# A 64-state selective scan on one core: y's sums in 64x64 tiles, odd states with exchanged halves, carries copied on GpSimd, preparation one pair later

## The chip, the cores and the metric

The program runs on 1 core of a Trainium2 chip. The metric is the device time of one execution in microseconds (us). The engines of the core work through queues of their own and wait for each other by semaphores: PE (TensorE, matmuls), DVE (VectorE), ACT (ScalarE), POOL (GpSimd), and SP, which only issues transfers. PEld is the loading of weights into PE.

## The reference

The network is four layers on x of shape 4 x 128 x 64 x 64: a sparse attention, a selective scan with 64 states, a rank-one attention and a two-way scan with 16 states. The change is in the second layer, whose core, per sample (L = 4096 positions, C = 128 channels, n = 64 states), is this:

```python
xproj = xp @ W_in                              # u and the convolution's input
...                                            # layer norm of u with gamma, beta
dt, B_, C_ = split(u @ W_dt)                   # 8 + 64 + 64 columns
delta = softplus(dt @ W_dtr + b_dtr)
a = exp(delta[..., None] * A)                  # A = -exp(A_log), one value per channel and state
h[l] = a[l] * h[l-1] + delta[l] * B_[l] * u[l] # for each of 64 states
y[l] = sum over states of C_[l, n] * h[l, :, n]  + D * u[l]
y = y + silu(conv) * ...                       # gated 3x3 depthwise convolution
out = y @ W_out + x
```

## The kernel before, in words

Channels lie on the 128 partitions, positions along the free dimension. The scan layer (`scan_layer`, L455 on) takes the 16384 positions of the four samples in 16 **chunks** of 1024 (index K; four to a sample), and in each chunk the 64 states one after the other. A state in a chunk is a **unit**; two units, an even and an odd one, are a **pair** (index k, 0 to 31). Every engine runs an unrolled program written pair by pair, so the order of each queue is the order of its source.

For each pair:

- ACT makes `decay` for the two units: exp(delta * A), one 128x1024 activation each (L829), and scales eight blocks of the transposed `duT` by the odd unit's B (L842), giving `xt`.
- PE broadcasts the even unit's row of B to all partitions with one-hot weights `sel` (L668, `broadcast_B`) and transposes `xt` back (L678, `turn_back`). DVE multiplies the broadcast B by `du` in place (L1036, `even_input`).
- DVE scans the even and the odd unit (L1049, 2.3 us each), reading the input from PSUM and writing `h`. In three chunks of four it then copies the last column of each `h` into `carry` (L1055, `keep`), from which the next chunk's scan of that state starts.
- SP loads the unit's row of C, broadcast to 128 partitions, into one of `CS` = 5 slots of `hc`; POOL multiplies it by `h` (L951, `product`).
- PE adds the product into `y_sum` (two PSUM banks) with an identity matrix as weights (L688, `add_state`): two 128x512 float32 matmuls a unit, which the profile shows as four. PE adds the products of the pair before the one that DVE is at.

Between these, each engine prepares the next chunk in pieces, tied to k: PE projects u (L566, k = 0, 1), POOL squares it into `usq` (L914, k = 1), PE sums the squares over channels with eight one-column matmuls (L573, `prep_var`, k = 4), DVE and ACT make the reciprocal root (L990 to L1000, L758, L760, k = 4), PE broadcasts it (L583, k = 5, 6), DVE scales u (L1005, k = 5, 6), and further projections, delta's softplus on ACT and POOL (POOL's four steps after pairs 18 to 21) and the transposed du follow. The finished chunk is closed by `add_y` (L1023, DVE, after the scans of pair 0 of the next chunk), the gating (L1017), `add_conv` (L946, POOL, after pair 2), the projection (L659) and the residual (L1029). PE also makes the 3x3 convolution in 18 pieces between pairs (L644).

PE's wait for the squares stands ahead of everything that follows it in PE's queue: the sums and the broadcast of B for the next pair.

The fourth layer (`two_way_scan_layer`) is a scan of the same shape with 16 states. It already forms y's sums in four 64x64 tiles (L1545, `add_pair`), takes exp(delta * A) of the odd states from a copy of delta with exchanged halves (`crossed`), and keeps carries on DVE (L1927).

Of the kernel before, what the change touches and what calls it, by code (L numbers as in the profile page):

```python
# [454 lines left out]
def scan_layer(nc, x, w, sel, weights_in, conv_weights):  # L455
# [11 lines left out]
    HS, DS, CS, XS = 4, 4, 5, 4  # L467
    ctx = ExitStack()
    with ctx:
# [12 lines left out]
        delta = sb("delta", [128, 2, CH])  # L482
        du = sb("du", [128, 2, CH])
# [7 lines left out]
        part = sb("part", [PARTS * SEL, CH], BF16)  # L491
        z1, z2 = sb("z1", [128, CH]), sb("z2", [128, CH])
        z3, rows_sb = usq, z1[0:S1, :]
        carry = sb("carry", [128, S1])
# [27 lines left out]
        c_in = [sem(f"c_in_{i}") for i in range(CS)]  # L522
        hc_done = sem("hc_done"); sum_mm = sem("sum_mm"); y_out = sem("y_out"); yg_ready = sem("yg_ready")
# [15 lines left out]
        def _(sp):  # L539
# [11 lines left out]

            sp.dma_start(conv_raw, conv_weights).then_inc(conv_in, 16)
            store_rows(0)
            for K in range(NCH):
                for q in range(S1):
                    load_row(K, q)
                    if q == 26 and K + 1 < NCH:
                        store_rows(K + 1)

        @block.tensor  # L560
        def _(pe):
# [99 lines left out]
            def broadcast_B(P, p):  # L661
# [49 lines left out]
            for K in range(NCH):  # L711
                p = K % 2
                for k in range(PAIRS):
                    P = K * PAIRS + k
                    turn_back(P)
                    if P:
                        add_state(2 * P - 2)
                    if k in CONV:
                        convolution(K, *CONV[k])
                    if K + 1 < NCH:  # L720
                        if k < 2:
                            prep_u(K + 1, k)
                        if k == 4:
                            prep_var(K + 1)
                        if k in (5, 6):
                            prep_rstd(K + 1, k - 5)
# [16 lines left out]
            for unit in range(NCH * S1 - 2, NCH * S1):  # L743
                add_state(unit)
# [4 lines left out]
        def _(act):  # L749
# [25 lines left out]
            def split_high(K):  # L775
                act.wait_ge(bdt_out, 2 * K + 2)
                nc.scalar.activation(part[:], rest[0:PARTS * SEL, :], ACT.Identity,
                                     scale=w[0:PARTS * SEL, L1_AT["below_top"]][:, 0:1]).then_inc(part_ready, 1)

            def split_middle(K):  # L780
                act.wait_ge(rest_ready, K + 1)
                nc.scalar.activation(part[:], rest[0:PARTS * SEL, :], ACT.Identity,
# [22 lines left out]
            def soft_log(K):  # L805
# [3 lines left out]
                nc.scalar.activation(z3[:], z3[:], ACT.Identity, bias=wt("minus_one")).then_inc(exp_ln, 1)  # L809
                nc.scalar.activation(z2[:], z1[:], ACT.Ln, bias=1.0).then_inc(exp_ln, 1)  # L810

            def duT_copy(K, p, j):
                act.wait_ge(duT_mm, 2 * K + j + 1)
                nc.scalar.activation(duT[:, p, 4 * j:4 * j + 4, :].rearrange("p t d -> p (t d)"), prep_ps,
                                     ACT.Identity).then_inc(duT_out, 1)
# [8 lines left out]
            def decays(unit, p):  # L824
                K, q = divmod(unit, S1)
                if q == 0:
                    act.wait_ge(delta_ready, K + 1)
                at_least(act, scan_done, unit - DS + 1)
                nc.scalar.activation(decay[:, unit % DS, :], delta[:, p, :], ACT.Exp,  # L829
# [41 lines left out]
            for K in range(NCH):  # L871
                p = K % 2
                for k in range(PAIRS):
# [10 lines left out]
                    if K + 1 < NCH:  # L884
                        if k < 2:
                            u_copy(K + 1, 1 - p, k)
                        if k == 4:
# [1305 lines left out]
```

## Time and profile before

| | us |
|---|---|
| median of 3 runs (lowest, highest) | 10606.26 (10604.6, 10616.05) |
| the profiled execution: its own time | 10616.89 |
| its span | 10615.1 |
| the scan layer: first scan to the last `add_y` | 2838.8 to 5945.1 |

| engine | busy us | share of the span |
|---|---|---|
| PE | 9717.4 | 92% |
| DVE | 8515.8 | 80% |
| ACT | 8057.9 | 76% |
| POOL | 5905.9 | 56% |

Times in the rows are from the start of the span. The profiled execution is 10.6 us above the median; what is worked out from its rows is a difference and is laid on the median. Matmuls overlap one another, so their starts tell more than their durations; DVE's instructions overlap the one before by about 0.08 us. PEclk is the share of full speed that TensorE's clock was granted: 1.0 is 2.4 GHz, 0.5 is 1.2 GHz.

### The profile page before, as it was taken

How to read it: one execution, taken by the hardware profiler on the slowest of the kernel's cores; microseconds unless marked ns; L12 is line 12 of the kernel's file. 1: busy time of each engine (PE TensorE's matmuls, PEld its weight loads, DVE VectorE, ACT ScalarE, POOL GpSimd, SP SyncE). 2: the span in 40 equal slices, each digit the busy share in tenths (PEclk: the TensorE clock that was granted, in tenths of full speed). 3: DMA queues.
4: the chain of work that ended last, by engine and by line, in shares of the span. 5: the costliest groups of instructions: out<-in, count | busy, mean ns of one | idle time of the engine just before them, and what ended most of it. 6: DMA issues, size and time to landing. Idle time of an engine off the chain costs nothing. (4 is left out here: it accounts for less than half of the span.)

```text
span 10615.1 us, 137498 instructions
## 1 busy us (share of the span) xinstructions
PE 9717.4 (92%) x45956; PEld 5177.6 (49%) x45956; DVE 8515.8 (80%) x8102; ACT 8057.9 (76%) x14637; POOL 5905.9 (56%) x2628
## 2 busy tenths in 40 slices
PE   9999999999899999999999999988888888888885
PEld 6767767677444444444444444433333333333332
DVE  7858858578599999999999411159999999999997
ACT  5646646466488888888888555579999998888885
POOL 0000000000288888888888300058989988889885
PEclk9999999999899999999999999989999999999997
DMA  1000000000145555545555100035555555555556
GB/s 41 0 1 0 0 0 0 0 0 0 61 173 175 175 175 174 177 174 174 176 174 177 66 8 8 8 120 184 186 184 179 187 182 189 184 186 188 183 187 220
DMA packets 335957, 1241.58 MB, mean 117 GB/s; under 512 B 38672, under 2 KB 38800, under 8 KB 331792
## 3 DMA queue, kind: packets, MB, share of 16 engines
q1 hardware_dynamic: 335472, 1235.51, 34.7%
q8 instruction: 256, 4.19, 0.2%
q14 instruction: 229, 1.88, 0.1%
HBM read 1145.18 MB, written 56.62 MB: 113 GB/s over the span
## 5 line engine op out<-in xcount | busy, mean ns | idle before, releaser
L951 POOL TENSOR_TENSOR l_hc<-l_h,l_hc 128x1024 f32<-128x1024 f32 x1024 | 2398.8, 2365 | 451.5 <-DVE l_h L1049 451.0
L1841 POOL TENSOR_TENSOR l_ring<-l_ring 128x1024 f32<-128x1024 f32 x1024 | 2429.7, 2397 | 347.4 <-DVE l_ring L1919 341.3
L1919 DVE TENSOR_TENSOR_SCAN l_ring<-l_ring,l_carry,l_ps 128x1024 f32<-128x1024 f32 x960 | 2200.1, 2333 | 1.3
L688 PE MATMUL l_ps<-l_hc,w_sb 128*128 128x512 f32 x4096 | 1936.4, 595 | 69.1 <-POOL l_hc L951 61.7
L1049 DVE TENSOR_TENSOR_SCAN l_h<-l_decay,l_carry,l_ps 128x1024 f32<-128x1024 f32 x768 | 1760.3, 2334 | 4.3 <-issue 0.4
L1545 PE MATMUL l_ps<-l_ring,w_sb 64*64 64x512 f32 x8192 | 1216.9, 667 | 343.0 <-POOL l_ring L1841 334.4
L116 POOL COPY l_qm<-l_q 128x128 f32 x128 | 82.7, 648 | 2576.4 <-PE l_ps L188 2179.5
L829 ACT ACTIVATE l_decay<-l_delta,w_sb 128x1024 f32<-128x1024 f32 x1024 | 1152.8, 1138 | 168.8 <-DVE l_h L1049 168.6
L1731 ACT ACTIVATE l_xt<-l_duT,l_BT 128x128 f32<-128x128 f32 x4096 | 1246.0, 388 | 0.0
L842 ACT ACTIVATE l_xt<-l_duT,l_BT 128x128 f32<-128x128 f32 x4096 | 1245.9, 388 | 0.0
L212 PE MATMUL l_ps<-l_attnT,l_vT 128*128 128x128 f32 x8192 | 1095.7, 277 | 1.3 <-ACT l_attnT L283 1.3
L212 PEld LDWEIGHTS l_ps<-l_attnT,l_vT 128*128 128x128 f32 x8192 | 1013.9, 192 | 138.0 <-issue 114.7
L188 PE MATMUL l_ps<-l_k,l_qm 128*128 128x512 f32 x2048 | 1055.0, 599 | 16.7 <-DVE l_E L395 16.6
L688 PEld LDWEIGHTS l_ps<-l_hc,w_sb 128*128 128x128 f32 x4096 | 735.3, 190 | 659.6 <-issue 491.8
L1184 PE MATMUL l_ps<-l_E,l_hs 128*128 128x512 f32 x2048 | 880.0, 592 | 5.2 <-DVE l_hs L1250 5.2
L401 DVE SCALAR_TENSOR_TENSOR l_E<-l_relu,l_E 128x1024 f32<-128x1024 f32 x512 | 626.7, 1225 | 287.2 <-ACT l_E L276 287.2
L276 ACT ACTIVATE l_E<-l_E,l_offsets 128x1024 f32<-128x1024 f32 x512 | 587.0, 1146 | 290.5 <-DVE l_E L395 290.4
L270 ACT ACTIVATE l_relu<-l_ps,l_offsets 128x1024 f32<-128x1024 f32 x512 | 570.8, 1115 | 272.6 <-PE l_ps L188 270.8
L1211 ACT ACTIVATE l_E<-l_g,l_neg_max,l_f 128x4096 f32<-128x4096 f32 x128 | 486.4, 3800 | 380.2 <-PE l_ps L1184 368.3
L1903 DVE TENSOR_TENSOR l_ps<-l_du,l_ps 128x1024 f32<-128x1024 f32 x512 | 622.2, 1215 | 179.9 <-PE l_ps L1518 178.4
L1528 PEld LDWEIGHTS l_ps<-w_sb,l_xt 128*128 128x128 f32 x4096 | 479.0, 150 | 556.4 <-DVE l_ring L1919 385.0
L201 PEld LDWEIGHTS l_ps<-w_sb,l_E 128*128 128x128 f32 x4096 | 507.1, 141 | 409.8 <-issue 392.7
(233 smaller groups left out, 15001.6 us busy)
## 6 DMA issues: line engine op xcount, KB each, us to landing
l_hc<-l_rows_dram SPq DMA_DIRECT2D x1024, 512.0 KB, 3.7
l_ring<-l_rows_dram SPq DMA_DIRECT2D x1024, 512.0 KB, 4.8
l_crossed<-l_delta SPq DMA_DIRECT2D x128, 256.0 KB, 5.3
l_gate_dram<-l_gate SPq DMA_DIRECT2D x32, 512.0 KB, 7.1
l_recon_dram<-l_recon SPq DMA_DIRECT2D x32, 512.0 KB, 5.4
l_gate<-l_gate_dram SPq DMA_DIRECT2D x32, 512.0 KB, 6.0
l_xw<-x_dram SPq DMA_DIRECT2D x30, 513.5 KB, 7.3
x_dram<-x SPq DMA_DIRECT2D x16, 512.0 KB, 2.6
```

Source lines behind the costliest of these rows:

```text
L188: ins = nc.tensor.matmul(logits[c % 2][:, j * BANK:(j + 1) * BANK], qm[:, h, :], k[:, c * CH + j * BANK:c * CH + (j + 1) * BANK], start=Tr ...
L212: ins = nc.tensor.matmul(ps[:, bank, 0:128], vT[:, t * 128:(t + 1) * 128], attnT[:, g % 2, j * 128:(j + 1) * 128], start=t == 0, stop=t == ...
L688: ins = nc.tensor.matmul(y_sum[:, half(j)], ident, hc[:, unit % CS, half(j)], start=q == 0, stop=q == S1 - 1)
L829: nc.scalar.activation(decay[:, unit % DS, :], delta[:, p, :], ACT.Exp, scale=wt("A")[:, q:q + 1]).then_inc(decay_ready, 1)
L842: ins = nc.scalar.activation(xt[:, (2 * P + hf) % XS, t * 128:(t + 1) * 128], duT[:, p, blk, :], ACT.Identity, scale=BT[:, p, blk, k:k + 1])
L951: nc.gpsimd.tensor_tensor(hc[:, unit % CS, :], h[:, unit % HS, :], hc[:, unit % CS, :], ALU.mult).then_inc(hc_done, 1)
L1049: nc.vector.tensor_tensor_scan(h[:, unit % HS, :], decay[:, unit % DS, :], odd_in if odd else even_in, before, ALU.mult, ALU.add).then_inc ...
L1184: ins = nc.tensor.matmul(ps[:, j, :], hs[:, s, :], E[:, s, j * BANK:(j + 1) * BANK], start=start, stop=stop)
L1545: ins = nc.tensor.matmul(ps[to, 4 + j, :], ident[own, own], hc[own, (2 * P + odd) % CS, half(j)], start=r == 0 and phase == 0, stop=r == P ...
L1731: ins = nc.scalar.activation(xt[:, (2 * P + hf) % XS, t * 128:(t + 1) * 128], duT[:, S % 2, 4 * hf + t, :], ACT.Identity, scale=BT[:, K % ...
L1841: nc.gpsimd.tensor_tensor(hc[:, unit % CS, :], h[:, unit % HS, :], hc[:, unit % CS, :], ALU.mult).then_inc(hc_done, 1)
L1919: nc.vector.tensor_tensor_scan(h[:, unit % HS, order], decay[:, unit % DS, order], x_now[:, order], before, ALU.mult, ALU.add).then_inc(sc ...
```

## The change

1. **y's sums.** `add_state` becomes `add_pair(P, phase)`. Each of its two phases issues four 64x64-tile matmuls of 64x512, one for each combination of input half and output half of the partitions, for both units of a pair. The odd unit's halves are exchanged, so that its channels 0 to 63 lie on partitions 64 to 127. The sums are two pairs late instead of one, and `hc` has 7 slots instead of 5.
2. **Exchanged halves.** The decay of odd units comes from `crossed`, a copy of delta with exchanged halves that SP makes with two transfers of 256 KB a chunk (`cross_delta`, queued behind the row load of unit 62); `duT_copy` writes exchanged halves; A's odd columns are rolled by 64.
3. **Carries** are copied by POOL, ahead of each product, instead of by DVE.
4. **Preparation.** PE's and ACT's pieces for u move from k = 0, 1 to 2, 3; POOL's squares from after pair 1 to after pair 4; `prep_var`, `rstds` and `newton` from 4 to 5; the scaling by one; `add_y` from after pair 0 to after pair 1 and `add_conv` from after pair 2 to after pair 3.
5. **sel** keeps one column a state and is read with a stride of 0 for the 128 columns of weights, in the scan layer and in the fourth layer. `part` shares memory with `z2`, with two more waits on ACT for that.

```diff
-    HS, DS, CS, XS = 4, 4, 5, 4
+    HS, DS, CS, XS = 4, 4, 7, 4
...
+            def cross_delta(K):
+                sp.wait_ge(delta_ready, K + 1)
+                at_least(sp, decay_ready, S1 * K)
+                for side in range(2):
+                    sp.dma_start(crossed[64 * side:64 * side + 64, :],
+                                 delta[64 - 64 * side:128 - 64 * side, K % 2, :]).then_inc(crossed_in, 16)
...
-                    ins = nc.tensor.matmul(even_in[:, half(j)], sel[:, k * 128:(k + 1) * 128], stack[:, p, half(j)],
+                    ins = nc.tensor.matmul(even_in[:, half(j)], sel[:, k:k + 1].broadcast_to([PARTS * SEL, 128]), stack[:, p, half(j)],
...
-            def add_state(unit):
-                K, q = divmod(unit, S1)
-                if q == 0:
-                    at_least(pe, y_out, K)
-                pe.wait_ge(hc_done, unit + 1)
-                for j in range(2):
-                    ins = nc.tensor.matmul(y_sum[:, half(j)], ident, hc[:, unit % CS, half(j)], start=q == 0,
-                                           stop=q == S1 - 1)
-                ins.then_inc(sum_mm, 1)
+            def add_pair(P, phase):
+
+                K, k = divmod(P, PAIRS)
+                if phase == 0:
+                    if k == 0:
+                        at_least(pe, y_out, K)
+                    pe.wait_ge(hc_done, 2 * P + 2)
+                    at_least(pe, sum_mm, 2 * P)
+                else:
+                    pe.wait_ge(first_half_mm, P + 1)
+                lower, upper = slice(0, 64), slice(64, 128)
+                for own, other, j in ((lower, upper, phase), (upper, lower, 1 - phase)):
+                    for odd, to in enumerate((own, other)):
+                        ins = nc.tensor.matmul(ps[to, 4 + j, :], ident[own, own], hc[own, (2 * P + odd) % CS, half(j)],
+                                               start=k == 0 and phase == 0, stop=k == PAIRS - 1 and phase == 1)
...
                     turn_back(P)
-                    if P:
-                        add_state(2 * P - 2)
...
-                        if k < 2:
-                            prep_u(K + 1, k)
-                        if k == 4:
+                        if k in (2, 3):
+                            prep_u(K + 1, k - 2)
+                        if k == 5:
                             prep_var(K + 1)
...
+                    if P > 1:
+                        add_pair(P - 2, 0)
                     if P + 1 < NCH * PAIRS:
                         broadcast_B(P + 1, p if k + 1 < PAIRS else 1 - p)
-                    if P:
-                        add_state(2 * P - 1)
...
+                    if P > 1:
+                        add_pair(P - 2, 1)
...
             def product(unit):
+                K, q = divmod(unit, S1)
+                pool.wait_ge(scan_done, unit + 1)
+                if K % NC < NC - 1:
+                    nc.gpsimd.tensor_copy(carry[:, q:q + 1], h[:, unit % HS, CH - 1:CH]).then_inc(kept, 1)
                 pool.wait_ge(c_in[unit % CS], 16 * (unit // CS) + 16)
-                pool.wait_ge(scan_done, unit + 1)
...
-                    if k == 2 and K:
+                    if k == 3 and K:
                         add_conv(K - 1)
                     if K + 1 < NCH:
-                        if k == 1:
+                        if k == 4:
                             squares(K + 1, 1 - p)
```

PE's queue around the squares' sum, before, in the first chunk: pairs 3 to 5. L688 are the sums of y, L668 the broadcast of B, L678 the transposes, L573 the squares' sum.

```order
L678 MATMUL l_ps<-w_sb,l_xt 128x128 x8
L688 MATMUL l_ps<-l_hc,w_sb 128x512 x2
L573 MATMUL l_ps<-w_sb,l_usq 128x1 x8
L668 MATMUL l_ps<-l_stack,sel 128x512 x2
L688 MATMUL l_ps<-l_hc,w_sb 128x512 x2
L678 MATMUL l_ps<-w_sb,l_xt 128x128 x8
```

The same place after: L690 are the transposes, L585 the squares' sum, L707 the sums of y, L680 the broadcast of B.

```order
L690 MATMUL l_ps<-w_sb,l_xt 128x128 x8
L585 MATMUL l_ps<-w_sb,l_usq 128x1 x8
L707 MATMUL l_ps<-l_hc,w_sb 64x512 x4
L680 MATMUL l_ps<-l_stack,sel 128x512 x2
L707 MATMUL l_ps<-l_hc,w_sb 64x512 x4
```

The squares' sum now stands in the group of pair 5 (before: of pair 4), and behind it both phases of a pair's sum enclose the broadcast of B.

POOL's queue from the end of the first chunk into the second, before: L951 are products, L914 squares u, L946 is `add_conv`.

```order
L951 TENSOR_TENSOR l_hc<-l_h,l_hc 128x1024 x24
L914 TENSOR_TENSOR l_usq<-l_u 128x1024
L951 TENSOR_TENSOR l_hc<-l_h,l_hc 128x1024 x2
L946 TENSOR_TENSOR l_yg<-l_yg,l_cg 128x1024
```

The same after, from the products of pair 3 of the second chunk: L979 copies a carry, L981 is a product, L973 `add_conv`, L941 the squares.

```order
L979 COPY l_carry<-l_h 128x1
L981 TENSOR_TENSOR l_hc<-l_h,l_hc 128x1024
L979 COPY l_carry<-l_h 128x1
L981 TENSOR_TENSOR l_hc<-l_h,l_hc 128x1024
L973 TENSOR_TENSOR l_yg<-l_yg,l_cg 128x1024
L979 COPY l_carry<-l_h 128x1
L981 TENSOR_TENSOR l_hc<-l_h,l_hc 128x1024
L979 COPY l_carry<-l_h 128x1
L981 TENSOR_TENSOR l_hc<-l_h,l_hc 128x1024
L941 TENSOR_TENSOR l_usq<-l_u 128x1024
```

Before, the squares come behind pair 1 and three pairs ahead of the pair in which PE asks for them; after, they come behind `add_conv` and pair 4, one pair ahead.

DVE's queue at the start of the second chunk, before: L1049 are scans, L1036 `even_input`, L1055 the copies of carries, L1023 `add_y`.

```order
L1049 SCALAR_TENSOR_TENSOR l_h<-l_decay,l_carry,l_ps 128x1024 x2
L1023 SCALAR_TENSOR_TENSOR l_yg<-l_u,w_sb,l_ps 128x1024
L1036 TENSOR_TENSOR l_ps<-l_du,l_ps 128x1024
L1055 COPY l_carry<-l_h 128x1 x2
L1049 SCALAR_TENSOR_TENSOR l_h<-l_decay,l_carry,l_ps 128x1024 x2
```

After: L1079 are scans, L1066 `even_input`, L1053 `add_y`, L1047 the gating.

```order
L1079 SCALAR_TENSOR_TENSOR l_h<-l_decay,l_carry,l_ps 128x1024 x2
L1066 TENSOR_TENSOR l_ps<-l_du,l_ps 128x1024
L1079 SCALAR_TENSOR_TENSOR l_h<-l_decay,l_carry,l_ps 128x1024 x2
L1053 SCALAR_TENSOR_TENSOR l_yg<-l_u,w_sb,l_ps 128x1024
L1066 TENSOR_TENSOR l_ps<-l_du,l_ps 128x1024
L1047 SCALAR_TENSOR_TENSOR l_cg<-l_ps,w_sb,l_cg 128x512
```

`add_y` stands one pair later, and the copies of carries are gone from DVE.

## Rows read from the trace of the kernel before

**Rows 1.** Stretches: length, busy us of each engine, PEclk, DMA.

```profile
2838.00:5945.00 3107.00, 2971.46 (x10930) 1527.59 (x10930) 3046.91 (x2500) 2626.25 (x5546) 2657.90 (x1144) 1.00 0.51 174
7012.00:10530.00 3518.00, 2956.94 (x15906) 1147.36 (x15906) 3292.42 (x2714) 3212.97 (x6215) 3133.73 (x1338) 0.94 0.57 184
```

**Rows 2.** DVE's waits in chunks 1 to 14: us, times, longest.

```profile
DVE l_ps L1036 <- PE l_ps L668: 22.8, 45, 0.9
DVE l_yg L1023 <- PE l_ps L688: 11.3, 15, 0.9
```

**Rows 3.** DVE in order of time, chunk 7: start, us, instruction, [idle before].

```profile
4203.86 1.28 DVE L1023 SCALAR_TENSOR_TENSOR l_yg<-l_u,w_sb,l_ps 128x1024 f32<-128x1024 f32 x1 [0.86 <-PE l_ps L688]
...
4206.32 4.58 DVE L1049 TENSOR_TENSOR_SCAN l_h<-l_decay,l_carry,l_ps 128x1024 f32<-128x1024 f32 x2
...
4212.59 4.58 DVE L1049 TENSOR_TENSOR_SCAN l_h<-l_decay,l_carry,l_ps 128x1024 f32<-128x1024 f32 x2
4217.08 1.21 DVE L1036 TENSOR_TENSOR l_ps<-l_du,l_ps 128x1024 f32<-128x1024 f32 x1
4218.33 4.59 DVE L1049 TENSOR_TENSOR_SCAN l_h<-l_decay,l_carry,l_ps 128x1024 f32<-128x1024 f32 x2
```

**Rows 4.** DVE, two pairs of chunk 6 between which two copies of carries stand.

```profile
4023.79 4.58 DVE L1049 TENSOR_TENSOR_SCAN l_h<-l_decay,l_carry,l_ps 128x1024 f32<-128x1024 f32 x2
...
4029.54 4.59 DVE L1049 TENSOR_TENSOR_SCAN l_h<-l_decay,l_carry,l_ps 128x1024 f32<-128x1024 f32 x2
```

**Rows 5.** POOL in order of time, chunk 7, from the products of pair 1.

```profile
4208.81 4.70 POOL L951 TENSOR_TENSOR l_hc<-l_h,l_hc 128x1024 f32<-128x1024 f32 x2 [3.23 <-DVE l_h L1049]
4213.46 1.90 POOL L914 TENSOR_TENSOR l_usq<-l_u 128x1024 f32<-128x1024 f32 x1
...
4219.97 2.35 POOL L946 TENSOR_TENSOR l_yg<-l_yg,l_cg 128x1024 f32<-128x1024 f32 x1
4222.29 9.29 POOL L951 TENSOR_TENSOR l_hc<-l_h,l_hc 128x1024 f32<-128x1024 f32 x4
```

**Rows 6.** PE at granted clock 1.0: the scan layer's squares' sum; layer four.

```profile
4226.52 1.84 PE L573 MATMUL l_ps<-w_sb,l_usq 128*128 128x1 f32 x16
4228.23 0.59 PE L668 MATMUL l_ps<-l_stack,sel 96*128 96x512 bf16 x2
...
7879.09 1.09 PE L1545 MATMUL l_ps<-l_ring,w_sb 64*64 64x512 f32 x8
7880.11 0.60 PE L1518 MATMUL l_ps<-l_stack,sel 96*128 96x512 bf16 x2
...
7881.66 1.09 PE L1528 MATMUL l_ps<-w_sb,l_xt 128*128 128x128 f32 x8
```

**Rows 7.** PE behind long gaps: layer four, and the squares' sum ahead of chunk 0.

```profile
2786.59 3.55 PE L573 MATMUL l_ps<-w_sb,l_usq 128*128 128x1 f32 x16 [2.75 <-POOL l_usq L914]
...
10390.96 1.98 PE L1545 MATMUL l_ps<-l_ring,w_sb 64*64 64x512 f32 x8 [4.62 <-POOL l_ring L1841]
10392.88 1.04 PE L1518 MATMUL l_ps<-l_stack,sel 96*128 96x512 bf16 x2
...
10395.76 1.75 PE L1528 MATMUL l_ps<-w_sb,l_xt 128*128 128x128 f32 x8
```

**Rows 8.** Small POOL instructions: in order of time, and one line's (ns min/median/max).

```profile
0.27 0.10 POOL L2186 MEMSET const-float32-1.0<- 128x1 f32 x1
...
L116 POOL COPY l_qm<-l_q x128: 291/541/4263, 22.6 to 2659.0; 128x128 f32 x128
```

**Rows 9.** Weight loads: layer four's sel (busy us, mean ns | idle before), and L170 (ns min/median/max).

```profile
L1518 PEld LDWEIGHTS l_ps<-l_stack,sel 96*128 96x128 bf16 x1024 | 59.4, 99 | 560.5 <-DVE l_ring L1919 307.5 <-issue 252.9
...
L170 PEld LDWEIGHTS l_ps<-w_sb,l_rinv x256: 185/190/192, 44.5 to 2123.4; 128*128 128x128 f32 x128
```

**Rows 10.** DMA issues of the page: count, KB each, median us to landing.

```profile
l_crossed<-l_delta SPq DMA_DIRECT2D x128, 256.0 KB, 5.3
```

More of the change, by code:

```diff
@@ L482, in scan_layer @@
         delta = sb("delta", [128, 2, CH])
+        crossed = sb("crossed", [128, CH])
         du = sb("du", [128, 2, CH])
@@ L558, in _ @@
                         store_rows(K + 1)
+                    if q == 62 and K + 1 < NCH:
+                        cross_delta(K + 1)
         @block.tensor
@@ L738, in _ @@
                         project(K - 1, k - 21)
+                    if P > 1:
+                        add_pair(P - 2, 0)
                     if P + 1 < NCH * PAIRS:
                         broadcast_B(P + 1, p if k + 1 < PAIRS else 1 - p)
-                    if P:
-                        add_state(2 * P - 1)
-            for unit in range(NCH * S1 - 2, NCH * S1):
-                add_state(unit)
+                    if P > 1:
+                        add_pair(P - 2, 1)
+            for P in (NCH * PAIRS - 2, NCH * PAIRS - 1):
+                for phase in range(2):
+                    add_pair(P, phase)
             for j in range(2):
@@ L776, in split_high @@
                 act.wait_ge(bdt_out, 2 * K + 2)
-                nc.scalar.activation(part[:], rest[0:PARTS * SEL, :], ACT.Identity,
+                at_least(act, low_ready, 2 * K)
+                nc.scalar.activation(part, rest[0:PARTS * SEL, :], ACT.Identity,
                                      scale=w[0:PARTS * SEL, L1_AT["below_top"]][:, 0:1]).then_inc(part_ready, 1)
@@ L781, in split_middle @@
                 act.wait_ge(rest_ready, K + 1)
-                nc.scalar.activation(part[:], rest[0:PARTS * SEL, :], ACT.Identity,
+                nc.scalar.activation(part, rest[0:PARTS * SEL, :], ACT.Identity,
                                      scale=w[0:PARTS * SEL, L1_AT["below_top"]][:, 1:2]).then_inc(part_ready, 1)
@@ L813, in duT_copy @@
                 act.wait_ge(duT_mm, 2 * K + j + 1)
-                nc.scalar.activation(duT[:, p, 4 * j:4 * j + 4, :].rearrange("p t d -> p (t d)"), prep_ps,
-                                     ACT.Identity).then_inc(duT_out, 1)
+                nc.scalar.activation(duT[:, p, 4 * j:4 * j + 4, :].rearrange("p t (s d) -> p t s d", s=2)[:, :, ::-1, :],
+                                     prep_ps.rearrange("p (t s d) -> p t s d", t=4, s=2), ACT.Identity).then_inc(duT_out, 1)
             def silu(K, j):
@@ L827, in decays @@
                     act.wait_ge(delta_ready, K + 1)
+                if q == 1:
+                    act.wait_ge(crossed_in, 32 * K + 32)
                 at_least(act, scan_done, unit - DS + 1)
-                nc.scalar.activation(decay[:, unit % DS, :], delta[:, p, :], ACT.Exp,
+                nc.scalar.activation(decay[:, unit % DS, :], crossed[:] if q % 2 else delta[:, p, :], ACT.Exp,
                                      scale=wt("A")[:, q:q + 1]).then_inc(decay_ready, 1)
@@ L1080, in _ @@
                     scan(P, 1)
-                    if k == 0 and K:
+                    if k == 1 and K:
                         add_y(K - 1, 1 - p)
@@ L1517, in broadcast_B @@
                     for j in range(2):
-                        ins = nc.tensor.matmul(even_in[:, half(j)], sel[:, r * 128:(r + 1) * 128], stack[:, K % 2, half(j)],
+                        ins = nc.tensor.matmul(even_in[:, half(j)], sel[:, r:r + 1].broadcast_to([PARTS * SEL, 128]), stack[:, K % 2, half(j)],
                                                start=True, stop=True)
@@ L2054, in network @@
         sem = lambda name: ctx.enter_context(nc.semaphore(name))
-        sel = ctx.enter_context(nc.sbuf_tensor("sel", [PARTS * SEL, SEL * 128], BF16))
+        sel = ctx.enter_context(nc.sbuf_tensor("sel", [PARTS * SEL, SEL], BF16))
         x_dram = nc.dram_tensor("x_dram", [C, B * N], F32, kind="Internal").ap()
@@ L2125, in layer1_arrays @@
                ("out_w", 0, W_out), ("ident", 0, _np.eye(128)), ("ones", 0, _np.ones((128, 1))),
-               ("A", 0, A_log[:, by_unit]), ("below_top", 0, below_top), ("minus_one", 0, _np.full((128, 1), -1)),
+               ("A", 0, _np.where(_np.arange(S1) % 2, _np.roll(A_log[:, by_unit], 64, 0), A_log[:, by_unit])),
+               ("below_top", 0, below_top), ("minus_one", 0, _np.full((128, 1), -1)),
                ("bdt_b", 0, column(_np.concatenate([b_dt[even_B]] * PARTS + [b_dt[:R1]]))),
@@ L2167, in one_hot_rows @@
 def one_hot_rows():
-    select = _np.zeros((PARTS * SEL, SEL, 128), _np.float32)
-    for a in range(PARTS):
-        for i in range(SEL):
-            select[a * SEL + i, i, :] = 1
-    return select.reshape(PARTS * SEL, SEL * 128).astype(mybir.dt.np(BF16))
+    return _np.concatenate([_np.eye(SEL)] * PARTS).astype(mybir.dt.np(BF16))
 def kernel(**inputs):
```

40 lines of the change are left out of this document (20 added, 20 removed).

## The prediction

> **What bounds the kernel now.** I read the stretches first [rows 1]: in the scan layer DVE is busy for 3047 of 3107 us, PE for 2971, POOL for 2658, and PE's clock is granted in full. DVE sets the pace, PE follows closely. Then DVE's own waits [rows 2]: in the 14 chunks 1 to 14 it waits 45 times for the broadcast of B (22.8 us) and 15 times for y's sums (11.3 us). Last, DVE in order of time: a plain pair takes 4218.33 - 4212.59 = 5.74 us from scan to scan [rows 3]. With two copies of carries in it, it takes 4029.54 - 4023.79 = 5.75 us [rows 4]: the copies lie in the time that the scan must wait for `even_input` anyway. So the engine that the change relieves most, PE, is not the bound; it can give back no more than the waits.
>
> **What the change can give.** Chunks 1 to 14: the recorded waits are 34.1 us. Each of these 60 also loses the 0.08 us by which DVE's instructions otherwise overlap, 4.8 us. Delays too short to be listed are some 0.5 us a chunk by the starts of chunk 7, 7 us. Without the copies, a gating, scaling or transposed copy can start 0.12 us earlier at six places in a chunk: 0.7 us in the 11 of these chunks that have copies, 8 us. Together 54 us. Chunk 0 has the same kinds of waits, 3.6 us; the last chunk's pairs run without a wait, so it gives nothing, and its tail pays 0.9 us since two pairs of sums are left instead of one. **Gain: 57 us**, if nothing new is late.
>
> The saving on PE is real but hidden. A phase of tile matmuls advances PE by 7880.11 - 7879.09 = 1.02 us [rows 6]. Two phases, a broadcast (0.6) and the transposes (1.09) make 3.7 of a pair's 5.74 us: 2 us are then idle, or 1 where a piece of preparation or convolution stands between.
>
> **What is late next: the squares.** POOL now squares u behind `add_conv` and the products of pair 4, and PE asks for it in pair 5, ahead of the sums and of the broadcast of B for pair 6. I follow a chunk without copies, from its first scan at 0. Pair 1 scans at 5.74. `add_y` (1.28 less 0.08 of overlap) now stands behind it, and the gating adds 4212.59 - 4206.32 - 5.74 = 0.53 [rows 3], so pair 2 scans at 5.74 + 5.74 + 1.20 + 0.53 = 13.21, pair 3 at 18.95, pair 4 at 24.69, pair 5 at 30.43. `even_input` for pair 6 would follow 4217.08 - 4212.59 = 4.50 later, **at 34.93**.
>
> POOL starts a pair's products 4208.81 - 4206.32 = 2.49 after its scans begin and takes 4213.46 - 4208.81 = 4.65 for the two [rows 3, 5]. Pair 3: 21.44 to 26.09. `add_conv` takes 4222.29 - 4219.97 = 2.32: to 28.41. Pair 4, whose first scan has long ended: to 33.06. Squares, 1.90: **34.96**. PE has had nothing to do since its transposes of pair 5, which end about 30.3: a gap of 4.7 us.
>
> Behind the squares stand, on the way to `even_input`: the squares' sum (1.71 from its start to the next, at full clock), a phase (1.02), the broadcast (0.60) [rows 6]. At full clock that ends at 38.3: a stall of 3.4 us.
>
> But after a gap of 4.62 us the fourth layer's phase took 1.98 us instead of 1.09 and the broadcast 1.04 instead of 0.60, and 4.8 us in, the transposes still took 1.75 instead of 1.09 [rows 6, 7]: PE ran at 1.2 GHz for some 6.3 us. Ahead of chunk 0, after a gap, the squares' sum itself took 3.55 us instead of 1.84 [rows 7]. With those, the chain is 3.45 + 1.92 + 1.03 = 6.40, which is about as long as the slow spell, and the last of it ends at 41.4: **a stall of 6.5 us**. If the clock came back after the squares' sum it would be 5.2. I take 6.5, since the gap is as long as the one in the row and one-column matmuls are the lightest work PE has here.
>
> **The copies on POOL** (price c each) delay the squares by four of them. The trace has no such copy. A 128x1 MEMSET on POOL takes 0.10 us; L116's copy of 128 columns has a median of 0.54 [rows 8]. I take 0.10, by the form that is nearest in size; the ends are 0.03 (the pitch at which the MEMSETs follow each other) and 0.54. In a plain pair POOL is idle for 5.74 - 4.65 = 1.09 us, so two copies cost DVE nothing there up to 0.54. So the stall in a chunk with copies is 6.5 + 0.4 = 6.9.
>
> The Trainium skill, GPSIMD Engine Reference, section Elementwise, side-by-side cycle accounting, gives DVE about 156 ns of dispatch an instruction and GpSimd two software hops where DVE has one. As an estimate from that page a copy would be near 0.31 us, and the sum would grow by 4 x 0.21 x 11 = 9 us; no trace here shows it.
>
> Chunk 0 has no `add_conv` and no `add_y`: its squares end 2.49 + 4.65 + 1.90 + 0.2 = 9.24 after pair 4's scans, the chain at 15.7, against 10.24 for `even_input`: 5.4 us. Chunk 15 prepares nothing. **Cost: 3 x 6.5 + 11 x 6.9 + 5.4 = 101 us.**
>
> **What is hidden.** POOL's four delta steps after pairs 18 to 21 each add 2.3 us to a pair that leaves 1.09 free: the products come 4.9 us late, 5.7 with the copies, less about 1 that DVE spends there itself. A product must be done when the scan four units on begins, 11.5 us after its own scan; begun at 2.5 and 2.3 long, it may be 6.7 late. That holds up to c of about 0.3. The two transfers for `crossed` land 5.3 us after issue [rows 10]. SP can issue them when the chunk's last decay is made; `decay` has four slots, so ACT makes that one nearly two pairs ahead of its scan, and the first decay that reads `crossed` is wanted by the scan two units further: 5.3 us within some 13. A row of C for an odd unit can only be asked for when the pair three before is summed, at about the start of its own pair, and is needed 6 us in: a landing like that of [rows 10] leaves 1 us. The new wait of `split_high` is for work of a chunk ago, that of the logarithm for a POOL step two pairs ago. The carries' wait is met two pairs early.
>
> The Trainium skill, TensorEngine Tiling (Array Packing), section Key Properties, says that changing the tiling mode drains TensorE. The change brings four such changes a pair. The rows differ: in layer four a broadcast starts 1.02 after the phase begins, as tightly as between equal forms [rows 6], so nothing is added for it.
>
> `sel` read with a stride of 0: a load of it takes 99 ns, a float32 load from a broadcast column 190 as any float32 load [rows 9]. I take no change. At worst 0.09 us on each of the fourth layer's 512 broadcasts, 46 us; where DVE does not wait for them, nothing.
>
> **Sum:** 101 - 57 = +44 us on the profiled execution's 10616.9; laid on the median of 10606.3: **10650 us**.
>
> **Rivals.**
> - *The clock stays up* (not slower). If PE's clock is not lowered in the gap, or is back at once, the chain is 3.3 us: 3 x 3.4 + 11 x 3.8 + 2.7 = 55 against 57: 10604 us. It decides below a stall of 3.8 us a chunk. For it: layer four's clock is granted at 0.94 on the whole [rows 1], so most of its gaps cost nothing. Against it: gaps of this length [rows 7].
> - *PE's wait for the squares binds nothing* (faster), if the squares are ready before 31: the gain of 57 alone, 10549 us. Against it: pair 4's second product can't start before 29.2 and squares 1.9 follow it. It would need POOL's order to be other than its source.
> - *Dear copies.* At c = 0.54 POOL needs 64 x (2.33 + 0.54) + 18 = 202 us a chunk (its two instructions by their pitch, 18 for the other steps) and becomes the bound, against 3107/16 = 194.2 now: 11 x 7.6 us and a few more, about +86 us, 10692. It begins to bind at c of about 0.3.
> - *Slower weight loads* from `sel`: up to 46 more, 10655 to 10696.
> - *A low clock in ordinary pairs.* PE is idle for 2 us in each, as in layer four. Where its clock falls, a pair with a piece of preparation needs about 7 us instead of 5.74; with two or three a chunk, +50 us: 10700. For it: 0.94 [rows 1]; against it, that the gaps are of 1.5 us.
>
> **How the numbers follow.** Forecast 0.56: 10650, itself from 10625 (clock back early) to 10665. Clock stays up 0.13. Faster 0.07. Dear copies 0.09. Weight loads 0.08. Low clock elsewhere 0.07. The range that holds 8 in 10 is 10602 to 10692: it leaves out the faster case and the upper parts of the last three. About 0.2% (21 us) is what a measurement of this kernel can tell from no change; above 10627 lie all of the forecast but 0.04 and the last three cases: slower 0.52 + 0.24 = 0.76; within 0.2%: 0.13 + 0.04 = 0.17; faster 0.07.
>
> **What would show it.** DVE's wait for the broadcast of B should be 15 waits of about 6.5 to 7 us (5.4 the first), all before pair 6, and nearly no others; the wait for y's sums gone. PE should wait some 4.7 us for POOL's squares, its sum take about 3.5 us and the granted clock there be 0.5. The copies on POOL should last about 0.1 us. PE's busy time in the scan layer should fall by hundreds of us to no effect. Stalls of 3.4 would refute the clock; none would refute the order; waits of DVE for POOL's products around pairs 20 to 24 would show dear copies; more of DVE's waits for B in layer four, slower loads.

## The result, and the profile after

The changed kernel takes 10643.03 us (median of 10 runs, 10636.49 to 10658.11), the kernel before 10604.69 us beside it (10 runs, 10598.11 to 10616.05): a ratio of 1.0036, 95% interval [1.0026, 1.0046]. It is slower by 38 us. The profiled execution has a span of 10656.0 us, 40.9 more than before.

The same two stretches as in [rows 1] (length, busy us of PE, PEld, DVE, ACT and POOL, PEclk, DMA):

```profile
2838.00:6000.00 3162.00, 2500.99 (x15046) 982.08 (x15045) 3017.68 (x1745) 2642.10 (x5553) 2752.84 (x1913) 0.96 0.53 174
7012.00:10570.00 3558.00, 2975.51 (x15958) 1161.00 (x15960) 3308.65 (x2716) 3232.12 (x6235) 3141.14 (x1343) 0.94 0.56 182
```

In the scan layer PE has lost 470 us of work, and the layer has become longer. DVE's waits in the first stretch say why (us, times, longest), beside those of [rows 2]:

```profile
DVE l_ps L1066 <- PE l_ps L680: 126.2, 17, 24.6
DVE l_tmp L1024 <- ACT l_root L783: 8.3, 15, 0.6
...
DVE l_yg L1053 <- PE l_ps L707: 5.3, 1, 5.3
```

The wait of 24.6 us stands ahead of the first scan, as before. The other 16 make 101.6 us: one of 0.38, and 15 that are one wait a chunk. The wait for y's sums is gone but for the last chunk's. PE in order of time, chunk 7 (start, us, instruction, [idle before]), for [rows 6, 7]:

```profile
4244.76 1.09 PE L690 MATMUL l_ps<-w_sb,l_xt 128*128 128x128 f32 x8 [0.61 <-DVE l_h L1079]
4250.44 3.54 PE L585 MATMUL l_ps<-w_sb,l_usq 128*128 128x1 f32 x16 [4.60 <-POOL l_usq L941]
4253.92 1.98 PE L707 MATMUL l_ps<-l_hc,w_sb 64*64 64x512 f32 x8
4255.84 1.03 PE L680 MATMUL l_ps<-l_stack,sel 96*128 96x512 bf16 x2
```

The granted clock in 4250.4 to 4258.0 is 0.50, that is 1.2 GHz, behind a gap of 4.60 us. POOL, for [rows 5], and DVE, for [rows 3], in the same chunk:

```profile
4236.80 4.70 POOL L981 TENSOR_TENSOR l_hc<-l_h,l_hc 128x1024 f32<-128x1024 f32 x2 [1.06 <-DVE l_h L1079]
4241.44 2.38 POOL L973 TENSOR_TENSOR l_yg<-l_yg,l_cg 128x1024 f32<-128x1024 f32 x1
4243.76 4.69 POOL L981 TENSOR_TENSOR l_hc<-l_h,l_hc 128x1024 f32<-128x1024 f32 x2
4248.38 1.92 POOL L941 TENSOR_TENSOR l_usq<-l_u 128x1024 f32<-128x1024 f32 x1
```

```profile
4245.86 4.58 DVE L1079 TENSOR_TENSOR_SCAN l_h<-l_decay,l_carry,l_ps 128x1024 f32<-128x1024 f32 x2
4256.91 1.23 DVE L1066 TENSOR_TENSOR l_ps<-l_du,l_ps 128x1024 f32<-128x1024 f32 x1 [6.46 <-PE l_ps L680]
4258.05 0.16 DVE L1020 TENSOR_SCALAR l_var<-l_ps 128x8 f32<-128x8 f32 x1
4258.76 0.17 DVE L1024 TENSOR_TENSOR l_tmp<-l_var,l_root 128x8 f32<-128x8 f32 x1 [0.55 <-ACT l_root L783]
4259.00 0.17 DVE L1026 TENSOR_TENSOR l_tmp<-l_tmp,l_root 128x8 f32<-128x8 f32 x1
```

POOL goes without a pause through the products of pair 3, `add_conv`, the products of pair 4 and the squares, which end at 4250.30; PE's chain behind them (the squares' sum, a phase of y's sums, the broadcast) ends at 4256.87, and only then can DVE make the input of pair 6.

In what follows, "the layer" is the time from the first scan of the scan layer to the start of its last `add_y`: 3106.3 us before, 3140.6 after, so +34.3. Until layer four's first scan it is then 4.0 us less, in layer four (first scan to last `add_y`) 8.4 us more. Layer four's code is the same in all the variants below that keep the change, and there it took from 3504.4 to 3527.6 us in the profiled executions, so the 8.4 is no finding.

The clock falls in ordinary pairs too. In 2838 to 5945 of the kernel before it was never below 1.0; in the same stretch after the change it is 0.50 for 232 us in all, and some 70 of them are not at a stall. In chunk 7, for example, it is 0.50 in 4232.1 to 4235.5, where PE had idled 2.25 us and then worked; the transposes there last 1.97 us. In the changed kernel DVE waits for none of this: outside the 15 stalls its only wait for the broadcast is the one of 0.38 us.

### The profile page after: what moved, and what is told of

Same layout as the page of the kernel before. It is cut to its first block and busy times, and to the rows that moved or that the text cites. A ratio compares the mean times of both kernels' runs of the same rounds, so it can differ in the third digit from the quotient of the medians.

```text
span 10656.0 us, 145495 instructions
## 1 busy us (share of the span) xinstructions
PE 9227.2 (87%) x50052; PEld 4629.1 (43%) x50052; DVE 8487.8 (80%) x7334; ACT 8068.5 (76%) x14637; POOL 5993.8 (56%) x3396
## 3 DMA queue, kind: packets, MB, share of 16 engines
q1 hardware_dynamic: 338032, 1243.12, 35.7%
q14 instruction: 225, 1.84, 0.1%
## 5 line engine op out<-in xcount | busy, mean ns | idle before, releaser
L981 POOL TENSOR_TENSOR l_hc<-l_h,l_hc 128x1024 f32<-128x1024 f32 x1024 | 2414.1, 2363 | 122.1 <-DVE l_h L1079 113.2
L1079 DVE TENSOR_TENSOR_SCAN l_h<-l_decay,l_carry,l_ps 128x1024 f32<-128x1024 f32 x768 | 1760.0, 2333 | 11.2
L707 PE MATMUL l_ps<-l_hc,w_sb 64*64 64x512 f32 x8192 | 1151.4, 633 | 2.7 <-POOL l_hc L981 2.2
L690 PE MATMUL l_ps<-w_sb,l_xt 128*128 128x128 f32 x4096 | 581.1, 287 | 281.6 <-DVE l_h L1079 279.5
L690 PEld LDWEIGHTS l_ps<-w_sb,l_xt 128*128 128x128 f32 x4096 | 456.2, 145 | 744.7 <-DVE l_h L1079 719.5
L856 ACT ACTIVATE l_decay<-l_delta,w_sb 128x1024 f32<-128x1024 f32 x512 | 586.2, 1145 | 248.7 <-DVE l_h L1079 247.4
L1925 DVE TENSOR_TENSOR l_ps<-l_du,l_ps 128x1024 f32<-128x1024 f32 x512 | 621.9, 1215 | 177.3 <-PE l_ps L1540 175.8
L1550 PEld LDWEIGHTS l_ps<-w_sb,l_xt 128*128 128x128 f32 x4096 | 481.1, 150 | 559.6 <-DVE l_ring L1941 382.4
```

Source lines behind the costliest of these rows:

```text
L690: ins = nc.tensor.transpose(odd_bank(hf)[:, t * 128:(t + 1) * 128], xt[:, (2 * P + hf) % XS, t * 128:(t + 1) * 128], ident)
L707: ins = nc.tensor.matmul(ps[to, 4 + j, :], ident[own, own], hc[own, (2 * P + odd) % CS, half(j)], start=k == 0 and phase == 0, stop=k == P ...
L981: nc.gpsimd.tensor_tensor(hc[:, unit % CS, :], h[:, unit % HS, :], hc[:, unit % CS, :], ALU.mult).then_inc(hc_done, 1)
L1079: nc.vector.tensor_tensor_scan(h[:, unit % HS, :], decay[:, unit % DS, :], odd_in if odd else even_in, before, ALU.mult, ALU.add).then_inc ...
```

## The experiments

In each, "the layer" and the waits are from the profiled execution of that kernel, and the ratio is to the kernel before on the same chip (its median there: 10609.22 us for the first four experiments, 10615.50 for the other four).

**POOL's squares ahead of pair 4's products.** The theory of the prediction: the late squares cost 101 us, and without them the gain is left.

```diff
-                    if k == 3 and K:
+                    if k == 4 and K:
                         add_conv(K - 1)
...
-                        if k == 4:
+                        if k == 3:
                             squares(K + 1, 1 - p)
```

> The changed kernel with two POOL steps exchanged: the squares come after the products of pair 3, add_conv after those of pair 4. Nothing else differs. Theory (DVE's 15 waits of 5.5 to 7.2 us for the broadcast of B are the squares, waited for by PE ahead of it): the squares now end 28.0 us after the chunk's first scan (21.4 + 4.65 + 1.9), before PE's transposes of pair 5 end at 30.3, so all 15 waits, 101 us, go, and what is left is the gain of 57 us against the kernel before: about 10545 us, 0.994 to 0.995 of before. Rival (PE has another reason to be late there, or the time returns elsewhere, at POOL's late products or the gap's low clock): waits of 2 us or more stay before pair 6, and the time stays above 10590.

Measured: 10586.25 us, ratio 0.9975 [0.9965, 0.9986]. The layer is 3085.2 us, 55.4 less than after the change; nearly the whole stall, 100 us, and a time of 10545 were expected. Apart from the 24.6, 12 waits for the broadcast of B are left with 10.6 us instead of 101.6, 91.0 less. Two of them, 2.26 us in chunk 0 and 2.28 in chunk 1, stand before pair 6 as the stalls did, though the squares are ready 2.8 us before PE takes them: the chain ran at 1.2 GHz there. In chunk 1 PE had no idle spell over 0.93 us in the 13 us ahead of it:

```profile
3055.98 0.61 PE L680 MATMUL l_ps<-l_stack,sel 96*128 96x512 bf16 x2 [0.93 <-DVE l_h L1079]
...
3058.22 1.84 PE L690 MATMUL l_ps<-w_sb,l_xt 128*128 128x128 f32 x8 [0.61 <-DVE l_h L1079]
3059.86 3.41 PE L585 MATMUL l_ps<-w_sb,l_usq 128*128 128x1 f32 x16
```

With 91.0 us less of waiting and a layer only 55.4 us shorter, 35.6 us came back elsewhere, on an instruction that the forecast had not looked at. DVE's groups in this kernel's scan layer (busy us, mean ns | idle before), then the same of after:

```profile
L1026 DVE TENSOR_TENSOR l_tmp<-l_tmp,l_root 128x8 f32<-128x8 f32 x15 | 28.2, 1877 | 1.1
L1024 DVE TENSOR_TENSOR l_tmp<-l_var,l_root 128x8 f32<-128x8 f32 x15 | 12.5, 833 | 8.3 <-ACT l_root L783 8.3
```

```profile
L1026 DVE TENSOR_TENSOR l_tmp<-l_tmp,l_root 128x8 f32<-128x8 f32 x15 | 2.5, 168 | 1.1
L1024 DVE TENSOR_TENSOR l_tmp<-l_var,l_root 128x8 f32<-128x8 f32 x15 | 2.5, 167 | 8.3 <-ACT l_root L783 8.3
```

`newton`'s first two instructions, eight columns each, take 40.7 us instead of 5.0: +35.7, and -91.0 + 35.7 = -55.3, against the layer's -55.4. They appear as busy, not as waiting. Chunk 7 of the swapped kernel, DVE and then POOL:

```profile
4226.00 0.46 DVE L1024 TENSOR_TENSOR l_tmp<-l_var,l_root 128x8 f32<-128x8 f32 x1 [0.55 <-ACT l_root L783]
4226.53 2.24 DVE L1026 TENSOR_TENSOR l_tmp<-l_tmp,l_root 128x8 f32<-128x8 f32 x1
4228.85 0.17 DVE L1028 TENSOR_SCALAR l_tmp<-l_tmp 128x8 f32<-128x8 f32 x1
```

```profile
4224.09 4.65 POOL L981 TENSOR_TENSOR l_hc<-l_h,l_hc 128x1024 f32<-128x1024 f32 x2
4231.72 4.68 POOL L981 TENSOR_TENSOR l_hc<-l_h,l_hc 128x1024 f32<-128x1024 f32 x2 [2.98 <-DVE l_h L1079]
```

POOL's two products end at 4226.43 and at 4228.74. DVE's first instruction ends at 4226.46, its second at 4228.77: each ends with the product that runs. `rstds`, just before them, takes its source from PSUM and writes SBUF, and lasts 0.15 us beside the same product: writing is not what waits. After the change DVE's instruction at 4258.76 comes where POOL has run out of scans to multiply, since DVE itself has stalled. In the kernel before, the last product of the run of four ends at 4222.29 + 9.29 = 4231.58 [rows 5], and newton's first instruction there at 4231.61:

```profile
4230.71 0.90 DVE L994 TENSOR_TENSOR l_tmp<-l_var,l_root 128x8 f32<-128x8 f32 x1 [0.55 <-ACT l_root L760]
```

**Carries copied by DVE again**, on top of that.

```diff
-                if K % NC < NC - 1:
-                    nc.gpsimd.tensor_copy(carry[:, q:q + 1], h[:, unit % HS, CH - 1:CH]).then_inc(kept, 1)
...
                         even_input(P + 1, p if k + 1 < PAIRS else 1 - p)
+                    if K % NC < NC - 1:
+                        keep(2 * P)
+                        keep(2 * P + 1)
```

> As e1_swap, but the copies of carries are on DVE again, two behind every even_input in three chunks of four, and not on POOL. Theory (a copy costs DVE nothing behind even_input in a plain pair, and 0.12 us where another instruction stands behind it, six times a chunk in 12 chunks): 8 to 9 us slower than e1_swap. Rival (768 copies of 0.10 us all lie on DVE's path): 79 us slower. Second rival (the copies loaded POOL enough to matter): faster than e1_swap.

Measured: 10585.04 us, ratio 0.9977 [0.9968, 0.9986]; the layer 3084.9 us, 0.3 less. The 8 to 9 us expected did not come: in the sum no difference shows. DVE's waits for the broadcast are 4.8 us less here (30.4 instead of 35.2) and newton's two instructions 6.5 less (34.2 instead of 40.7), so that some 11 us are lost elsewhere. Of these, 1.4 are a longer wait at the last `add_y`; the rest is of the order of what was expected for DVE's delayed side work, but is not located.

**y's sums untiled, two pairs late**, otherwise the swapped kernel: without the exchanged halves, `cross_delta` and the rolled A.

```diff
-                lower, upper = slice(0, 64), slice(64, 128)
-                for own, other, j in ((lower, upper, phase), (upper, lower, 1 - phase)):
...
+                pe.wait_ge(hc_done, 2 * P + phase + 1)
+                for j in range(2):
+                    ins = nc.tensor.matmul(y_sum[:, half(j)], ident, hc[:, (2 * P + phase) % CS, half(j)],
+                                           start=k == 0 and phase == 0, stop=k == PAIRS - 1 and phase == 1)
+                ins.then_inc(sum_mm, 1)
```

> As e1_swap, but y's sums are made with the whole identity, unit by unit as in the kernel before, and so no halves are exchanged and no delta is copied; the sums stay two pairs late with 7 slots, the copies stay on POOL. Theory (PE, at 5.4 us in a pair of 5.74 before any piece, has no room for a piece of about 1 us, and this is half of DVE's waits; the other half was PE waiting for POOL's products): DVE waits for B come back in pairs with two pieces and behind the squares' sum, 1 to 2 us a chunk, so 15 to 30 us slower than e1_swap, some 30 us faster than before. Rival A (the gain is the lateness alone): as fast as e1_swap. Rival B (the gain is the tiles alone): as slow as before.

Measured: 10621.38 us, ratio 1.0012 [1.0003, 1.0021]; the layer 3121.4 us, 36.2 more than with tiles. PE is busy for 3026 us in 2838 to 6000. Its waits, in that window:

```profile
DVE l_ps L1053 <- PE l_ps L677: 54.0, 44, 24.6
DVE l_yg L1040 <- PE l_ps L699: 9.2, 16, 6.5
```

63.2 us instead of 40.1 with tiles (35.2 and 4.9): +23.1. Newton's two are 46.0 instead of 40.7: +5.3. Of the 7.8 left, the 46 waits more would make 3.7 at the prediction's 0.08 us of lost overlap each, as an estimate; the rest is not located. Expected were 15 to 30 us more than with tiles and some 30 less than before; it is 36 more in the layer, and 12 more than before, where rival B (the gain is the tiles alone) put it. But part of that is newton, whose two instructions took 14.3 us in the kernel before. Without them the untiled layer would be 16.6 us under the layer before and the tiled one 47.5: about two thirds of the gain come with the tiles.

**The squares' sum at the end of pair 5 in PE's queue.** The other way to take the stall out: PE does not wait for the squares ahead of the sums and the broadcast.

```diff
-                        if k == 5:
-                            prep_var(K + 1)
...
                     if P > 1:
                         add_pair(P - 2, 1)
+                    if k == 5 and K + 1 < NCH:
+                        prep_var(K + 1)
```

> The changed kernel with one PE step moved: the squares' sum of pair 5 stands at the end of the pair, behind the sums and the broadcast of B, and no longer ahead of them. POOL's order is untouched. Theory: even_input no longer waits; PE's gap before the squares is about 1 us instead of 4.7, so its clock stays up and the sum takes 1.8 us instead of 3.5; the sum ends 36.9 us after the chunk's first scan (37.3 with copies), and DVE's rstds, which could start at 36.0, waits about 1 us. In all some 15 x 1.2 = 18 us instead of 102: about 10560 us. Rival (the low clock comes from the squares' sum itself, one-column matmuls, and not from the gap): the sum still takes 3.5 us and rstds waits about 2.8 us, about 10585 us.

Measured: 10587.17 us, ratio 0.9979 [0.997, 0.9989]; the layer 3086.7 us, 53.9 less than after. The waits:

```profile
DVE l_ps L1066 <- PE l_ps L680: 28.4, 9, 24.6
DVE l_var L1020 <- PE l_ps L585: 22.8, 15, 2.9
```

3.8 + 22.8 = 26.6 instead of 101.6: -75.0. Newton's two take 25.4 instead of 5.0: +20.4. Together -54.6, against -53.9. Here again the small instruction ends with POOL's product (4227.84 and 4227.82 in chunk 7). The time is that of the rival (10585, the sum always at 3.5 us), not the theory's 10560, but not for the rival's reason alone: the sum takes 1.92 to 2.96 us in twelve chunks and 3.27 to 3.55 in three, behind idle times of at most 1.1 us, and newton's 20.4 us were in neither account.

**Newton's values in PSUM, on top of the swapped kernel.** Two accounts of the long instructions are told apart: DVE waits for something that a GpSimd instruction holds when both of its sources are in SBUF, or for its own pipeline or ACT's write.

```diff
+        var_ps, tmp_ps = prep_ps[:, BLK:2 * BLK], prep_ps[:, 2 * BLK:3 * BLK]
...
-                nc.vector.tensor_tensor(tmp[:], var[:], root[:], ALU.mult)
+                nc.vector.tensor_tensor(tmp_ps, var_ps, root[:], ALU.mult)
                 dve.drain()
-                nc.vector.tensor_tensor(tmp[:], tmp[:], root[:], ALU.mult)
+                nc.vector.tensor_tensor(tmp_ps, tmp_ps, root[:], ALU.mult)
```

> The swapped kernel (squares after pair 3, gate sum after pair 4), with the newton step's small values (variance and its temporary, 128x8) kept in PSUM instead of SBUF, so that none of its four vector instructions reads two SBUF tensors. Theory, collision: in the swapped kernel one of newton's two first tensor_tensor instructions lasts until a GpSimd product that is running ends (its second one a median of 2.31 us instead of 0.17; chunk 7: begun 4226.53, ended 4228.77, the product ended 4228.74; the first one 0.46 us, ended 4226.46, the product before it 4226.41). Both together are 40.7 us of 15 chunks and would be 5. With PSUM as one source they run 0.17 to 0.2 us: the kernel comes out 30 to 36 us under the swapped one, about 10553. Rival, drain: the length is the wait for the vector engine's own pipeline or for ScalarE's write, and stays where the values lie in PSUM: 10586.

Measured: 10561.36 us, ratio 0.9946 [0.9933, 0.996]; the layer 3045.7 us, 39.5 less than the swapped kernel. About 10553 was expected. Both instructions are short:

```profile
L1027 DVE TENSOR_TENSOR l_ps<-l_ps,l_root 128x8 f32<-128x8 f32 x15 | 2.6, 175 | 1.1
L1025 DVE TENSOR_TENSOR l_ps<-l_ps,l_root 128x8 f32<-128x8 f32 x15 | 2.6, 175 | 7.8 <-ACT l_root L784 7.8
```

That is 35.5 of the 39.5; 3.5 more are waits for the broadcast (31.7 instead of 35.2). The drains and ACT's write are the same as before the edit, so they are not the cause. The fourth instruction, with one source in SBUF and its result in SBUF, takes 0.16 us beside a product too; so it is the two sources in SBUF that matter. From one `add_y` to the next, a chunk takes 189.8 to 191.4 us, the first and the last apart; after the change it was 196.4 to 197.2, before it 194.0 to 194.8. This is the fastest kernel of the study.

**The same edit in the kernel before.**

> The kernel before with that edit alone. Its newton's first instruction has a mean of 0.79 us against 0.17 for the three after it. Collision: 15 times 0.6, about 9 us less, 10600. Drain: no change, 10609.

Measured: 10604.76 us, ratio 0.9989 [0.998, 0.9998]; the layer 3096.5 us, 9.8 less. The instruction as it was before, and with the edit:

```profile
L994 DVE TENSOR_TENSOR l_tmp<-l_var,l_root 128x8 f32<-128x8 f32 x15 | 11.8, 790 | 8.6 <-ACT l_root L760 8.6
```

```profile
L995 DVE TENSOR_TENSOR l_ps<-l_ps,l_root 128x8 f32<-128x8 f32 x15 | 2.6, 175 | 8.1 <-ACT l_root L761 8.1
```

**The same edit in the changed kernel.**

> The changed kernel with that edit alone. There newton's instructions last 0.17 us each, since VectorE has stalled 6.9 us for the squares' sum just before and GpSimd has meanwhile run out of scans to multiply. Collision: nothing to gain, 10643 within 5 us. If PSUM operands were merely quicker or slower for small instructions, it would show here as a shift of up to 5 us either way.

Measured: 10648.29 us, ratio 1.0031 [1.0019, 1.0043]; the layer 3141.8 us, 1.2 more. As expected, there is nothing to gain where nothing collides, and a PSUM source is not itself quicker: 175 ns against 168.

**Fillers in the gap of the changed kernel.** PE multiplies something that nobody reads while it would wait for the squares.

```diff
+                for _ in range(5 if K else 0):
+                    nc.tensor.matmul(prep_ps, ident, u[:, K % 2, half(0)], start=True, stop=True)
                 pe.wait_ge(squared, K + 1)
```

> The changed kernel, with five matmuls whose result nobody reads put where TensorE waits for the squares (chunks 1 to 15), so that it is busy in the 4.6 us of the gap. Nothing that is computed changes. Theory, clock: the squares' sum then takes 1.84 us instead of 3.54, the group of tiled sums 1.09 instead of 1.98, the selection pair 0.6 instead of 1.0; the stall of VectorE goes from 6.9 to about 3.9 us, 15 times 3.0, so about 10598; less if newton, whose cover by the long stall shrinks, meets a GpSimd product again (up to 2.3 us a chunk, 10633). Rival, order: the length of the three instructions is that of their kind behind a wait, whatever ran before: no change, 10643, or later if the fillers outlast the squares.

Measured: 10618.38 us, ratio 1.0 [0.9991, 1.0009]; the layer 3109.1 us, 31.5 less than after, where about 45 were expected. The waits for the broadcast in the same window are 70.1 us instead of 101.6: the same 31.5. Chunks 7 and 8:

```profile
4228.40 4.46 PE L584 MATMUL l_ps<-l_u,w_sb 128*128 128x512 f32 x10
4233.08 1.95 PE L587 MATMUL l_ps<-w_sb,l_usq 128*128 128x1 f32 x16 [0.22 <-POOL l_usq L943]
4234.96 1.09 PE L709 MATMUL l_ps<-l_hc,w_sb 64*64 64x512 f32 x8
4235.98 0.60 PE L682 MATMUL l_ps<-l_stack,sel 96*128 96x512 bf16 x2
...
4421.84 4.46 PE L584 MATMUL l_ps<-l_u,w_sb 128*128 128x512 f32 x10
4426.98 1.95 PE L587 MATMUL l_ps<-w_sb,l_usq 128*128 128x1 f32 x16 [0.68 <-POOL l_usq L943]
4428.85 1.98 PE L709 MATMUL l_ps<-l_hc,w_sb 64*64 64x512 f32 x8
4430.77 1.04 PE L682 MATMUL l_ps<-l_stack,sel 96*128 96x512 bf16 x2
```

In both, the sum is short, as the clock theory says (1.95 us, in chunk 0 1.84, in two others 2.26 and 2.29). In chunk 7 the rest is at full clock too, and the stall is 3.45 us; in chunk 8 the clock is down behind the sum, and the stall is 5.24. The granted clock is 1.00 in 4228.4 to 4237.6 and 0.78 in 4425 to 4432. Of the 15 stalls, five lie between 3.45 and 3.96 us and ten between 4.39 and 5.61. Nine of the ten have the broadcast at the low clock; the tenth is chunk 0 (4.65), where the fillers outlast the squares by 2.3 us. What decides between the two kinds of chunk stays open. It is not the idle time ahead of the sum, 0.2 us in chunk 7 and 0.7 in chunk 8, since chunk 2 stays at full clock behind 0.73:

```profile
3260.34 1.95 PE L587 MATMUL l_ps<-w_sb,l_usq 128*128 128x1 f32 x16 [0.73 <-POOL l_usq L943]
3262.22 1.09 PE L709 MATMUL l_ps<-l_hc,w_sb 64*64 64x512 f32 x8
```

and chunk 3 falls behind 0.20, with a stall of 4.39. The rival, that the lengths belong to their kind and not to the clock, is refuted.

## Why the prediction was right, point by point

- **The squares are late, and the wait binds: right.** From pair 5's scans at 4245.86, `even_input` was due 4.50 later. The squares were worked out to end 0.03 behind that; they end at 4250.30, so 0.06 before it. The gap is 4.60 us against 4.7.
- **The clock falls, and the chain is 6.4 us: right.** 3.54, 1.98 and 1.03 us, with starts at 4250.44 and an end at 4256.87: 6.43. The stalls are 6.44 to 6.46 in the three chunks without copies (6.5), 6.91 to 7.15 in the eleven with copies (6.9), and 5.48 in chunk 0 (5.4). The sum is 101.2 us against 101. The filled gap shows what the low clock costs: 31.5 us with the clock up for a part of the chain only. The rival with the clock up (10604 us, 46 less) is thus refuted for the kernel as it is, and its price bounded from below. That it takes a gap to bring the clock down is not shown: in the swapped kernel it was down in chunks 0 and 1 without one of that length.
- **The copies at 0.10 us: right in the effect, by luck in the value.** A copy's record lasts a median of 183 ns, but chunks with copies stall 6.92 - 6.45 = 0.47 us longer: 0.12 for each of four. The estimate from the Trainium skill (GPSIMD Engine Reference, section Elementwise, side-by-side cycle accounting) was 0.31, more than either.
- **The gain of 57 us: 10 us too small, and the forecast of the net too high by as much.** The layer without its waits for B is 3140.6 - 101.6 = 3039.0, 67.3 under the layer before. Newton's first instruction went from 11.8 to 2.5 us: 9.3, which the prediction did not know. The rest is 58.0 against 57. So the net in the layer is 34.3 instead of 44; measured as medians, 38 us.
- **What was hidden stayed hidden from DVE.** The crossed transfers land after 5.2 us, those of C after 4.7 (before: 3.7). PE's 470 us less gave nothing beyond DVE's waits. The tiled sums start 1.0 us apart with the broadcast right behind them: no change of form costs anything that shows. `sel` loads in 98 ns in the scan layer and 99 in layer four, and layer four's waits for the broadcast are 175.8 us, before 178.4: the rival of slower loads is out. So is that of dear copies, by the 0.12 us. POOL and ACT do have new waits for the two transfers, which they had not before, but no wait of DVE for POOL or for a decay follows from them (us, times, longest):

```profile
POOL l_hc L981 <- DMA l_hc<-l_rows_dram: 8.6, 9, 1.1
ACT l_decay L856 <- DMA l_crossed<-l_delta: 8.5, 14, 1.3
```

- **The rival of a low clock in ordinary pairs: half right.** The clock does fall there (some 70 us), though the idle spell ahead of it in chunk 7 is of 2.25 us; but the 50 us that it priced did not come, since DVE does not wait at those places.
- **The rival "binds nothing" had the wrong number, and so had my expectation for the swapped kernel.** It gave 10549 us for a kernel whose squares come in time. The swapped kernel is that case, and has a ratio of 0.9975, which on 10604.69 is 10578. The sum had moved `newton` by a pair and taken its duration along, without asking what POOL would be doing at the new place. The step that failed is this term, put at nothing: the two instructions took 14.3 us before and take 40.7 in the swapped kernel, 26.4 more (35.7 more than in the changed kernel, where they take 5.0). With the collision taken away the ratio is 0.9946, 10547. For the forecast of the changed kernel the same omission cost only the 9.3 us named above, because the stall happened to keep the two apart: that part is luck.

The rule stands in the Trainium skill, SBUF — State Buffer, section Who interferes with whom: a vector instruction with two SBUF inputs takes the read port that it shares with GpSimd, and against a GpSimd instruction that reads SBUF whichever of the two starts second is blocked for the whole instruction of the other. The traces agree for DVE's side: in the kernel before and with the sum behind, all 15 long instructions end within 0.03 us of POOL's product, in the swapped kernel 25 within 0.07; and it is 175 ns once one input is in PSUM. The scans and `even_input` read one SBUF tensor of their size and one from PSUM, and keep a mean of 2333 and 1208 ns in the swapped kernel, none of them longer than 2349 and 1230. That a GpSimd instruction is held up by one of DVE's, no run here shows.

## What to carry to other kernels

Where work is moved, count the producer's queue up to the moved wait, and what the waiting engine has still to do behind it: squares that were ready just as VectorE's next input was due cost 6.5 us a chunk, since the sum, a phase and the broadcast were all still to come, at half the clock. Next, when a stall is taken out, ask what it had kept apart: here it had hidden a collision between tiny vector instructions and GpSimd's products. A small instruction that shows as busy for ten times the length of its kind may be waiting: compare its end with the ends of GpSimd's instructions. Here it helped to keep one of its two sources in PSUM.

## What the runs showed of the hardware

- An eight-column vector instruction with both sources in SBUF takes 0.17 us alone and up to 2.35 us beside a GpSimd product of 2.36 us; with one source in PSUM 175 ns beside the same products.
- Behind an idle spell of 4.6 us TensorE ran at 1.2 GHz (granted 0.50) for the whole of the next 6.4 us. With the spell filled down to 0.2 us the squares' sum took 1.95 us instead of 3.54, yet in chunk 8 the group behind it was at 1.98 again. In the swapped kernel the clock was down for such a chain (3.41 us for the sum) with no idle spell over 0.93 us in the 13 us ahead.
- A 128x1 GpSimd copy lasts 173 to 217 ns by its record and moved what stood behind it by some 0.12 us; the same copy on DVE lasts 147.
